# The first stage of a fused attention and feed-forward block, written out over its batches, with four slots for the split parts of q and k

## What is computed

```python
x = _layernorm(x + attn(x))      # 16 heads of width 8, causal, softmax of q k / sqrt(8), then W_o
x = _layernorm(x + ffn(x))       # silu(x Wg + bg) * (x Wu + bu) Wd + bd, plus a sum over experts
                                 # that two product-key top-8 searches pick per token and head
```

## Time and profile before

| | |
|---|---|
| median of 3 runs | 854.17 us (850.57, 854.17, 854.17) |
| the profiled execution's own time | 851.66 us |
| its span | 850.1 us |
| busy: PE, DVE, ACT, POOL | 738.5, 684.0, 567.2, 423.6 us |
| mean granted TensorE clock | 0.94 |
| moved by DMA | 67.06 MB, 79 GB/s over the span |

### The profile page before, as it was taken

How to read it: one execution, slowest core, us unless ns; L and a number is a source line. 1 busy time by engine, 2 the same in 40 slices (tenths; PEclk the granted TensorE clock), 3 DMA queues, 4 the chain that set the end, 5 groups by cost and what they waited for, 6 DMA issues and landing times. The chain is left out here.

```text
span 850.1 us, 17568 instructions
## 1 busy us (share of the span) xinstructions
PE 738.5 (87%) x4345; PEld 330.1 (39%) x4345; DVE 684.0 (80%) x2289; ACT 567.2 (67%) x926; POOL 423.6 (50%) x468
## 2 busy tenths in 40 slices
PE   6659899999999999999999998687788788887755
PEld 3332233333333333333333332233546455555345
DVE  5769999898998998989989890166888888888883
ACT  4440267666766676667666778558879798897771
POOL 8655111221122112211221123358999999999984
PEclk9885599999999999999999999997999999999997
DMA  6768535345543553355335330201001101100000
GB/s 174 225 159 200 113 73 120 83 94 125 120 86 84 126 125 80 88 124 126 81 86 123 83 81 23 89 2 52 1 3 36 38 1 38 37 1 13 4 11 25
DMA packets 58955, 67.06 MB, mean 79 GB/s; under 512 B 15488, under 2 KB 33536, under 8 KB 58880
## 3 DMA queue, kind: packets, MB, share of 16 engines
q1 hardware_dynamic: 53120, 62.35, 31.2%
q10 hardware_dynamic: 5184, 2.36, 1.0%
q0 software_dynamic: 576, 1.57, 0.7%
HBM read 46.73 MB, written 19.53 MB: 78 GB/s over the span
## 5 line engine op out<-in xcount | busy, mean ns | idle before, releaser
L698 ACT ACTIVATE probs<-ps 128x384 f32<-128x384 f32 (+2 forms) x384 | 290.9, 809 | 172.8 <-PE ps L752 170.7
L669 POOL TENSOR_SCALAR_AFFINE_SELECT probs<-probs 128x256 f32<-128x256 f32 x256 | 103.0, 407 | 361.4 <-ACT probs L698 359.0
L720 PE MATMUL ps<-Kx,Qx 128*128 128x512 bf16 (+3 forms) x768 | 233.0, 348 | 15.3 <-DVE mx L812 9.7
L808 DVE CUSTOM_DVE_ANT_0 junk<-ps,tri 128x256 bf16<-128x256 f32 (+3 forms) x512 | 228.2, 487 | 22.3 <-PE ps L720 18.8
L752 PE MATMUL ps<-Qa,Ka 128*128 128x512 bf16 (+3 forms) x768 | 180.3, 329 | 3.5 <-ACT probs L698 2.9
L812 DVE TENSOR_REDUCE mx<-ps 128x1 f32<-128x512 f32 x256 | 162.1, 681 | 13.8 <-issue 7.3
L738 PE MATMUL ps<-probs,Vg 128*9 128x512 f32 (+3 forms) x1536 | 153.3, 488 | 0.3 <-POOL probs L669 0.3
L720 PEld LDWEIGHTS ps<-Kx,Qx 128*128 128x128 bf16 x768 | 69.6, 98 | 207.0 <-DVE mx L808 85.8
L967 POOL TENSOR_TENSOR S<-sim 128x1024 f32<-128x1024 f32 x64 | 120.7, 1910 | 10.5 <-ACT sim L1030 5.4
L1219 DVE SCALAR_TENSOR_TENSOR A<-S,T,ps 128x511 f32<-128x511 f32 x128 | 90.1, 741 | 11.3 <-ACT ps L1041 9.4
L1041 ACT ACTIVATE ps<-S,nb 128x512 f32<-128x512 f32 x128 | 82.9, 680 | 11.4 <-DVE A L1219 10.8
(11 more groups left out here) (115 smaller groups left out, 862.6 us busy)
## 6 DMA issues: line engine op xcount, KB each, us to landing
Qx<-q_scr SPq DMA_DIRECT2D x48, 192.0 KB
Kx<-k_scr SPq DMA_DIRECT2D x48, 192.0 KB
Qa<-q_scr SPq DMA_DIRECT2D x48, 192.0 KB
Ka<-k_scr SPq DMA_DIRECT2D x48, 192.0 KB
o_scr<-Os SPq DMA_DIRECT2D x32, 256.0 KB, 2.2
q_scr<-qs SPq DMA_DIRECT2D x34, 128.0 KB, 3.2
k_scr<-qs SPq DMA_DIRECT2D x18, 128.0 KB, 3.1
xin<-in_L_attn_x_dram ACTq DMA_DIRECT2D x8, 256.0 KB, 3.8
```

The source lines that it names most:

```text
L669: pool.affine_select(out=diag, in_=diag, compare_op=ALU.is_ge, fill=0.0, base=0, pattern=[[0, 2], [1, P]], channel_multiplier=-1).then_inc ...
L698: act.activation(probs[:, k % 2, hh, 0:width], ps[:, bank:bank + 2, :].rearrange("p a c -> p (a c)")[:, 0:width], ACT.Exp, scale=SM_SCALE) ...
L720: pe.matmul(ps[:, X_BANK + f % X_SLOTS, 0:c1 - c0], Qx[:, u, hh, P * i:P * (i + 1)], Kx[:, u, hh, c0:c1], start=True, stop=True).then_inc( ...
L808: dve.tensor_tensor_reduce(out=junk[:, f % 4, 0:w], in0=src, in1=tri[:, CHUNK - w:CHUNK], scale=1.0, scalar=-BIG, op0=ALU.add, op1=ALU.max ...
```

## The change

`qs` gets four slots, and chunk n uses slot n % 4, with a semaphore per slot for SP's stores and for POOL's. The loops over batches of all five engines are written out, so that waits compare with constants and the `ONE` offsets of `qk_stored`, `v_ready` and `p3_made` go. ACT waits for stores only from chunk 4 on, for those of chunk n - 4; so does POOL. `qf`, `rf`, `xin` and `xT` keep two slots. ACT gets a wait for `r_made` of chunk n - 2 before it overwrites `qf`, and DVE's wait for `p3_made` now names chunk n - 2 and its own w. The sets of instructions and transfers that do the work are the same. In the attention block the stores of chunks 6 and 7 name their new slots, `6 * 16` becomes `LOADS * 16` with `LOADS = 6`, and nothing else is changed.

```diff
@@ -77,9 +77,12 @@
...
+QS = 4
+LOADS = 6
@@ -202,8 +205,8 @@
...
-        qk_stored = [sem(f"qk_stored{u}") for u in range(2)]
-        p3_stored = [sem(f"p3_stored{u}") for u in range(2)]
+        qk_stored = [sem(f"qk_stored{u}") for u in range(QS)]
+        p3_stored = [sem(f"p3_stored{u}") for u in range(QS)]
@@ -285,7 +288,7 @@
...
-        qs = operands.enter_context(nc.sbuf_tensor("qs", [P, 2, 2, PARTS, CHUNK], BF16))
+        qs = operands.enter_context(nc.sbuf_tensor("qs", [P, QS, 2, PARTS, CHUNK], BF16))
@@ -309,17 +312,17 @@
...
                 sp.wait_ge(p2_made, 4 * b + 2 * u + 2)
+                slot = (2 * b + u) % QS
                 for s in (0, 1, 3, 4):
-                    sp.dma_start(q_part(b, u, s), qs[:, u, 0, s % PARTS, :]).then_inc(qk_stored[u], 16)
+                    sp.dma_start(q_part(b, u, s), qs[:, slot, 0, s % PARTS, :]).then_inc(qk_stored[slot], 16)
                 for s in (0, 1):
-                    sp.dma_start(k_part(b, u, s), qs[:, u, 1, s, :]).then_inc(qk_stored[u], 16)
+                    sp.dma_start(k_part(b, u, s), qs[:, slot, 1, s, :]).then_inc(qk_stored[slot], 16)
@@ -361,11 +364,11 @@
...
-                    with sp.Fori(0, BATCH - 1) as b:
+                    for b in range(BATCH - 1):
...
-                        sp.wait_ge(qk_stored[u], STORES * 16 + ONE)
+                        sp.wait_ge(qk_stored[u], STORES * 16)
@@ -385,26 +388,21 @@
                     pool.memset(Kx[:], 0.0).then_inc(pads_made, 1)
-                    def third_parts(b, store=True):
+                    for b in range(BATCH):
                         for u in range(2):
-                            if not isinstance(b, int) or b > 0:
-                                pool.wait_ge(p3_stored[u], 32 * b)
+                            n = 2 * b + u
+                            if b > 1:
+                                pool.wait_ge(p3_stored[n % QS], 32)
                             for w in range(2):
-                                pool.wait_ge(p2_made, 4 * b + 2 * u + w + 1)
-                                pool.tensor_tensor(qs[:, u, w, 2, :], rf[:, u, w, :], qs[:, u, w, 1, :],
+                                pool.wait_ge(p2_made, 2 * n + w + 1)
+                                pool.tensor_tensor(qs[:, n % QS, w, 2, :], rf[:, u, w, :], qs[:, n % QS, w, 1, :],
                                                    ALU.subtract).then_inc(p3_made, 1)
-                            if not store:
-                                continue
-                            pool.wait_ge(p3_made, 4 * b + 2 * u + 2 + ONE)
-                            pool.dma_start(q_part(b, u, 2), qs[:, u, 0, 2, :]).then_inc(p3_stored[u], 16)
-                            pool.dma_start(k_part(b, u, 2), qs[:, u, 1, 2, :]).then_inc(p3_stored[u], 16)
-                    third_parts(0)
-                    with pool.Fori(1, BATCH - 1) as b:
-                        third_parts(b)
-                    third_parts(BATCH - 1, store=False)
+                            if b < BATCH - 1:
+                                pool.wait_ge(p3_made, 2 * n + 2)
+                                pool.dma_start(q_part(b, u, 2), qs[:, n % QS, 0, 2, :]).then_inc(
+                                    p3_stored[n % QS], 16)
+                                pool.dma_start(k_part(b, u, 2), qs[:, n % QS, 1, 2, :]).then_inc(
+                                    p3_stored[n % QS], 16)
                 @block.scalar
                 def _(act):
@@ -428,29 +426,27 @@
                     act.wait_ge(wqkv_loaded, 64)
                     act.sem_inc(q_read, 2 * FREE)
-                    def first_parts(b, more):
+                    for b in range(BATCH):
                         for u in range(2):
-                            if more:
-                                act.wait_ge(xT_ready, 2 * b + u + 1)
-                                act.dma_start(xin[:, u, :, :], x_chunks[bass.ds(2 * b + u + 2, 1)].rearrange(
-                                    "c p t d -> (c p) t d")).then_inc(x_loaded[u], 16)
-                            act.wait_ge(xT_read, 2 * b + u + 1 + FREE)
-                            act.activation(xbT[:, 2 * b + u, :] if isinstance(b, int) else
-                                           xbT[:, bass.ds(2 * b + u, 1), :].rearrange("p c t -> p (c t)"),
-                                           xT[:, u, :], ACT.Identity, bias=bo_col[:, 0:1]).then_inc(xb_made, 1)
-                            act.wait_ge(qk_stored[u], STORES * 16 * b + ONE)
+                            n = 2 * b + u
+                            if b < BATCH - 1:
+                                act.wait_ge(xT_ready, n + 1)
+                                act.dma_start(xin[:, u, :, :], x_chunks[n + 2]).then_inc(x_loaded[u], 16)
+                            act.wait_ge(xT_read, n + 1 + FREE)
+                            act.activation(xbT[:, n, :], xT[:, u, :], ACT.Identity, bias=bo_col[:, 0:1]).then_inc(xb_made, 1)
+                            if b > 1:
+                                act.wait_ge(qk_stored[n % QS], STORES * 16)
                             for w in range(2):
-                                act.wait_ge(qk_ready, 4 * b + 2 * u + w + 1)
+                                act.wait_ge(qk_ready, 2 * n + w + 1)
+                                if b > 0:
+                                    act.wait_ge(r_made, 2 * (n - 2) + w + 1)
                                 act.activation(qf[:, u, w, :], ps[:, 2 + 2 * w + u, :], ACT.Identity,
                                                bias=bqk[:, w:w + 1])
-                                act.activation(qs[:, u, w, 0, :], ps[:, 2 + 2 * w + u, :], ACT.Identity,
+                                act.activation(qs[:, n % QS, w, 0, :], ps[:, 2 + 2 * w + u, :], ACT.Identity,
                                                bias=bqk[:, w:w + 1]).then_inc(q_read, 1)
-                    with act.Fori(0, BATCH - 1) as b:
-                        first_parts(b, True)
-                    first_parts(BATCH - 1, False)
                     for n, (bank, dst) in enumerate(((1, WoC[:, :]), (2, downT[:, :]), (3, WqT[:, :, :]),
                                                      (4, kbd[:, :, :]), (5, Wsim[:, :, :]))):
                         turned_weights(n + 2, bank, dst)
@@ -489,7 +485,7 @@
...
-                    with pe.Fori(0, BATCH - 1) as b:
+                    for b in range(BATCH - 1):
@@ -528,9 +524,9 @@
...
-                        if not isinstance(b, int) or b > 0:
...
-                            dve.wait_ge(v_ready, n - 1 + ONE)
+                        if b > 0:
...
+                            dve.wait_ge(v_ready, n - 1)
@@ -540,14 +536,15 @@
                             dve.wait_ge(q_read, 2 * n + w + 1 + 2 * FREE)
-                            dve.wait_ge(p3_made, 4 * b + ONE)
-                            dve.tensor_tensor(rf[:, u, w, :], qf[:, u, w, :], qs[:, u, w, 0, :],
+                            if b > 0:
+                                dve.wait_ge(p3_made, 2 * (n - 2) + w + 1)
+                            dve.tensor_tensor(rf[:, u, w, :], qf[:, u, w, :], qs[:, n % QS, w, 0, :],
                                               ALU.subtract).then_inc(r_made, 1)
                             dve.wait_ge(r_made, 2 * n + w + 1)
-                            dve.tensor_copy(qs[:, u, w, 1, :], rf[:, u, w, :]).then_inc(p2_made, 1)
-                        dve.wait_ge(v_ready, n + 1 + ONE)
+                            dve.tensor_copy(qs[:, n % QS, w, 1, :], rf[:, u, w, :]).then_inc(p2_made, 1)
+                        dve.wait_ge(v_ready, n + 1)
                         for t in range(TPC):
-                            dst = vaug[:, bass.ds(b * HG, HG), TPC * u + t, :, 0:DH]
+                            dst = vaug[:, b * HG:(b + 1) * HG, TPC * u + t, :, 0:DH]
                             last = dve.tensor_tensor(dst, ps[:, 6 + u, P * t:P * (t + 1)].rearrange(
                                 "p (g h d) -> p g h d", g=HG, d=DH), bv_row[:].rearrange(
                                 "p (g h d) -> p g h d", g=HG, d=DH), ALU.add)
@@ -555,7 +552,7 @@
...
-                    with dve.Fori(0, BATCH - 1) as b:
+                    for b in range(BATCH - 1):
@@ -597,15 +594,19 @@
...
-                        sp.wait_ge(p3_made, 4 * (BATCH - 1) + 2 * u + 2 + ONE)
-                        sp.dma_start(q_part(BATCH - 1, u, 2), qs[:, u, 0, 2, :]).then_inc(qk_stored[u], 16)
-                        sp.dma_start(k_part(BATCH - 1, u, 2), qs[:, u, 1, 2, :]).then_inc(qk_stored[u], 16)
+                        sp.wait_ge(p3_made, 4 * (BATCH - 1) + 2 * u + 2)
+                        sp.dma_start(q_part(BATCH - 1, u, 2), qs[:, (2 * BATCH - 2 + u) % QS, 0, 2, :]).then_inc(
+                            qk_stored[(2 * BATCH - 2 + u) % QS], 16)
+                        sp.dma_start(k_part(BATCH - 1, u, 2), qs[:, (2 * BATCH - 2 + u) % QS, 1, 2, :]).then_inc(
+                            qk_stored[(2 * BATCH - 2 + u) % QS], 16)
...
```

(16 more changed lines are left out.)

## The result

| | before | changed |
|---|---|---|
| median | 852.6 us (6 runs, 850.57 to 854.17) | 842.7 us (6 runs, 841.19 to 845.6) |
| profiled execution, its span | 851.66, 850.1 | 842.8, 841.1 |
| first attention matmul | 61.44 | 52.70 |

The ratio of the times is 0.9889, with a 95% interval of 0.9866 to 0.9912: 9.5 us less, between 7.5 and 11.4. Three more runs of "before" than stood ahead of the prediction moved its median from 854.17 to 852.6.

The account below looks back on a forecast made before the run. ACT's wait for k stores, a closed loop through two slots, bounds the first stage. Attention starts at 53.1 instead of 61.4: 8.3 us off 851.66 gives 843.4, and 1.0 for the executions' mean makes about 844.3 us, range 839.7 to 849.2.

Parts of the forecast that it names:

- The store wait goes, all six instances: First stage: with four slots, ACT's 18.1 us in six waits for stores of k parts would all be gone.
- Loops written out, 0: All engines' batch loops: writing them out gains 0, with 1.1 us as upper bound, since few instruction packets were fetched.
- The pace, 4.65 us: First stage: time per chunk once the store wait goes, between DVE's 4.50 and POOL's 4.69 us; 5.9 before.
- The loads are the new wait: Head of attention: group 0 loads, issued at 44.6, make the first matmul wait 1.6 us or more, until 53.1.
- The tail of PE: End of first stage: TensorE's chain from the last activations at 42.9 lets the next block begin at 50.5 to 51.5.
- the lower figure: End of first stage: 50.5 us for the next block's start, with TensorE's tail at 2.4 GHz some 1 us shorter.
- POOL starved by DVE: Rival, first stage: DVE holds up POOL's store issues; at 6.8 us a chunk 4.3 us slower, about 858; chance 0.04.
- The DMA engines as a near tie: First stage: a chunk's 1.31 MB takes 4.4 to 4.7 us, as much as the engines; delays landing, not issue.
- The rest is a plain shift: After attention's start: everything moves earlier by the 8.3 us gained; a clock change is worth 1 to 2 us either way.

Follow-up runs that it names:

- two-slot run: Changed kernel with qs put back to two slots and the loops still written out; 850.03 us, ratio 0.9965 to before.

## Why the prediction was right

The forecast was 844.3 us, in a range of 839.7 to 849.2; measured were 842.7. The mechanism was as forecast; two of its terms were off and cancelled, and about 3 us of the gain have no term in it. By its own steps:

- *The store wait goes, all six instances.* Right: no row of ACT behind a store is left. The two-slot run shows that for the start of attention it was this and not the loops.
- *Loops written out, 0.* Right for the start (62.50 us against 62.43). But the two-slot kernel was 3.0 us faster than "before", and the sum has no term for that. No run shows where it comes from.
- *The pace, 4.65 us.* Measured 4.35. The term was over-sized at two places. On DVE I added the full length of the xT copy, but the next subtraction starts 0.60 us after it begins (25.92 to 26.52), not 0.68; that is 4.42 in place of 4.50. And on POOL I kept the 0.72 us issue as what it would pay beside a busy DVE; all issues from chunk 1 on took 0.53, 0.19 less. Chunk 2's subtraction was due at 23.1 and began at 22.16, since the whole stage had begun 0.9 us sooner, and chunk 7's was due at 45.7 and began at 43.33.
- *The loads are the new wait.* Right in kind, and it decided the start: predicted at 53.1, measured at 52.70. Two errors cancelled in it, and that is luck. The first load was issued at 42.31 in place of 44.6, but it took 10.4 us from there to PE's start and not 8.5. Of these 1.9 us about 1.0 are the release and PE's start after the last byte, which I had left out, and 0.3 are the last bytes of the old kernel, which I had put at the middle of a window that they filled; the remaining 0.6 fit a slower load, which this trace doesn't show by itself. The old kernel's spare time, by the same reading (bytes to 59.5, 0.6 us to the release, 0.4 to PE, against 61.44), was therefore 0.9 us and not 2.2. The other two profiles of the changed kernel started at 53.93 and 56.38, so that the mean of the three is 54.3, later than forecast. The experiment that moved the loads shows that the wait was real and how much of it could be had back.
- *The tail of PE.* The next block was to begin at 50.5 to 51.5 and began at 49.3, since the last activations began at 40.91 and not at 42.9. The distance, 8.4 us, fits the forecast's 7.6 to 8.6, but not by its path. The tail at full clock was 1.3 us shorter, as the lower figure assumed: 6.9 us from the last activations to the end of the last copy, 8.2 before. But POOL's last subtraction ended 0.2 us after that copy, and the block began 1.3 us after it, where it had begun 0.3 us after ACT's copy in the old kernel. The prediction didn't look at POOL there; what fills the 1.3 us no run shows.
- *POOL starved by DVE.* Not seen. The page SBUF — State Buffer of the Trainium skill, section SBUF: two separate sides, says that a DVE operation with two SBUF inputs and a POOL operation that reads SBUF exclude each other, and that a DVE operation in a two-port mode and any POOL operation do so too. The trace agrees for the operations: DVE's first subtraction of chunk 7, which has two inputs and began at 43.33 while POOL's subtraction ran until 43.85, took 1.07 us in place of 0.68. The cast took 1.27 us in place of 0.43 behind POOL's subtraction, and the run without that subtraction gave the difference back; which mode the cast ran in no row shows. The same page of the Trainium skill describes a trap in which DVE keeps POOL from issuing DMAs. Here no POOL issue beside the uninterrupted DVE was over 0.53 us after chunk 0's, so that trap did not close. The old trace already had an issue of 0.53 us at 47.87 beside DVE's subtraction from 47.90 on, so that the prediction's "0.53 us where DVE stands idle" did not hold for all of them.
- *The DMA engines as a near tie.* Right, and nearer than the text made it: full for 15 us. It did not hold the pace with four slots. With three slots ACT waited 6.6 us for stores, and without POOL's work 3.6 us.
- *The rest is a plain shift.* Right to 0.1 us in the first pair of profiles, which is in part luck: the other two profiles of the changed kernel have 785.4 and 786.2 us after the first row maximum in place of 787.7. Over the three, the start gained 7.5 us on average and not 9.0. The medians moved by 9.9, the profiled spans of the first pair by 9.0; the last block alone varies by more than that difference.

## What to carry to other kernels

A wait that closes a loop through a store (compute, issue, land, compute) is priced from the issue to the landing, and the slots that it takes are counted with the transfers at full load, not at the old pace: three slots looked enough, and ACT still waited 6.6 us for stores. When a stage is shortened, look at what its last transfers must deliver to the next one: a load that had barely been in time behind the stores became a wait of 5.5 us, and moving it ahead of two chunks of stores that nobody waited for was worth half as much again as the change itself had brought. A load's end is its release, not its last byte.

## What was not expected of the hardware

- Six loads that moved their bytes in 9.0 us released their waiter about 0.6 us after the last byte, in both profiles in which no other load was under way; a plain reading of the DMA share leaves this out.
- Where POOL's subtraction was the last work of the stage, the next block began 1.3 us after it; where ACT's copy was clearly the last, in the old kernel, 0.3 us after it.
- Between three profiles of one kernel, whose issues of the first load lay 0.7 us apart, the first matmul behind the loads started at 52.70, 53.93 and 56.38 us. The cause is open.
- With the DMA engines at a share near 1.0, SP's four store issues took up to 3.3 us in place of 2.5 (3.7 in the runs with three slots and without third parts): full transfers went with slower issues.
